# An adaLN transformer block on one core: key-tile sums wholly on GpSimd, earlier loads, and a new order in the first group and the finish

## What is computed

```python
mod = (silu(c) @ wmod).reshape(4, 6, 1, -1)
sa, ca, ga, sb, cb, gb = (mod[:, i] for i in range(6))
ga = sign(ga) * maximum(abs(ga), 0.25)          # gb likewise
h = layernorm(x) * (1 + ca) + sa
x = x + ga * attention(h)                       # causal, softmax(q k / sqrt(32)) v, then Wo and bo
h = layernorm(x) * (1 + cb) + sb
logits = h @ router_w.T                         # 4 experts, the best 2 kept, softmax
x = x + gb * sum_e gate_e * 4 * (h @ A_e.T) @ B_e.T
```

## Time and profile before

| | us |
|---|---|
| median of 3 runs (2901.94 to 2903.45) | 2902.95 |
| the profiled execution | 2904.26 |
| its span | 2902.5 |
| busy: TensorE, VectorE, GpSimd, ScalarE | 2772.0, 1583.7, 1281.9, 1060.7 |
| first attention group from, second from | 1229.5, 1286.4 |
| finish from | 2380.2 |

### The profile page before, as it was taken

The page is one execution under the profiler, slowest core; times in us unless marked ns, Lnnn a source line. Parts: engine busy times, 40 slices in busy tenths (PEclk is TensorE's granted clock), DMA queues, the critical chain, the costliest instruction groups (busy, mean ns, idle before and its releaser), DMA issues. The chain is left out here.

```text
span 2902.5 us, 41782 instructions
## 1 busy us (share of the span) xinstructions
PE 2772.0 (96%) x16195; PEld 2009.4 (69%) x16195; DVE 1583.7 (55%) x3171; ACT 1060.7 (37%) x1449; POOL 1281.9 (44%) x671
## 2 busy tenths in 40 slices
PE   5999999999999999879999999999999978999997
PEld 3888888888888888745555555555555547888886
DVE  4232233222322122267777787888778746777775
ACT  1322222232213111146555566666655641112121
POOL 3322332233224211157777777777777761112120
PEclk8999999999999999979999999999999989999998
DMA  7544354545334644355555555555555545554541
GB/s 250 183 158 159 139 203 166 177 158 190 128 116 149 214 174 175 112 119 125 126 126 124 127 123 121 118 121 119 121 121 128 136 173 142 144 156 136 162 131 58
DMA packets 171709, 421.58 MB, mean 145 GB/s; under 512 B 22204, under 2 KB 74548, under 8 KB 170232
## 3 DMA queue, kind: packets, MB, share of 16 engines
q1 hardware_dynamic: 139240, 298.03, 30.3%
q10 hardware_dynamic: 32272, 120.88, 18.9%
HBM read 278.77 MB, written 139.56 MB: 144 GB/s over the span
## 5 line engine op out<-in xcount | busy, mean ns | idle before, releaser
L1185 ACT ACTIVATE prob<-ps_s 128x1024 f32<-128x1024 f32 (+3 forms) x768 | 597.6, 810 | 415.5 <-PE ps_s L1361 399.8
L846 PE MATMUL ps_u<-h_hi,w_hi 128*128 128x512 f32 x1536 | 612.3, 399 | 1.8 <-POOL h_lo L586 1.8
L846 PE MATMUL ps_u<-h_lo,w_hi 128*128 128x512 f32 x1536 | 600.8, 391 | 0.0
L846 PE MATMUL ps_u<-h_hi,w_lo 128*128 128x512 f32 x1536 | 599.7, 390 | 0.0
L1139 POOL TENSOR_TENSOR added<-added,prob 128x2048 f32<-128x2048 f32 (+1 forms) x128 | 551.5, 4308 | 4.6
L580 POOL TENSOR_TENSOR w_lo<-w_raw,w_hi 128x1024 fp32r<-128x1024 f32 x93 | 222.6, 2393 | 478.4 <-ACT w_hi L648 478.4
L719 DVE SCALAR_TENSOR_TENSOR qk_lo<-ps_u,bias_col,qk_hi 128x512 fp32r<-128x512 f32 x128 | 96.0, 750 | 578.7 <-ACT qk_hi L624 578.7
L1242 DVE TENSOR_REDUCE part_high<-ps_r 128x1 f32<-128x512 f32 x496 | 330.4, 685 | 91.0 <-PE ps_r L1331 90.6
L1238 DVE CUSTOM_DVE_ANT_0 ps_r<-ps_r,row_mask 128x384 f32<-128x384 f32 (+1 forms) x500 | 312.1, 630 | 105.4 <-PE ps_r L1331 104.7
L1331 PE MATMUL ps_r<-k_st,q_st 96*128 96x512 f32 (+1 forms) x1008 | 331.9, 387 | 23.0 <-DMA v_sb<-v_tok 9.5
L846 PEld LDWEIGHTS ps_u<-h_lo,w_hi 128*128 128x128 f32 x1536 | 288.6, 188 | 61.8
(11 more groups left out here) (192 smaller groups left out, 3437.0 us busy)
## 6 DMA issues: line engine op xcount, KB each, us to landing
w_raw<-w_cols SPq DMA_DIRECT2D x72, 512.0 KB, 6.3
qk_split<-qk_hi SPq DMA_DIRECT2D x64, 512.0 KB, 2.6
qk_split<-qk_lo SPq DMA_DIRECT2D x64, 512.0 KB, 4.0
q_st<-qk_split ACTq DMA_DIRECT2D x60, 512.0 KB, 7.5
k_st<-qk_split ACTq DMA_DIRECT2D x60, 512.0 KB, 13.7
xn<-in_L_attn_x SPq DMA_DIRECT2D x8, 2048.0 KB, 11.2
v_tok<-v_out SPq DMA_DIRECT2D x32, 512.0 KB, 4.4
wm<-in_L_wmod SPq DMA_DIRECT2D x8, 2048.0 KB, 8.9
```

The lines of the kernel that those rows point to most:

```text
L846: last = nc.tensor.matmul(ps_u[u % 2][:], w[:, m, k], h[:, k, tok], start=k == 0 and j == 0, stop=k == KT - 1 and j == 2)
L1185: nc.scalar.activation(prob[:, buffer_of(t, k), 2 * pair:2 * pair + 2, off:], ps_s[pair][:, :, off:], ACT.Exp, scale=SCALE).then_inc(exp_d ...
```

## The change

`ADDS` becomes 7: GpSimd adds all eight upper key tiles, the adds of tiles 6 and 7 strewn between the masks 9, 10 and 11, and `sum_high` has only the matmuls on `added`. In the last group only 4 adds are made (`LAST_ADDS`), and matmuls take tiles 5 to 7. Group 1's queries and keys get a place of their own in the room of the projection weights and are loaded in the last group of `project`, the queries at its start, the keys behind the value store. `attend` then loads only values, and `FIRST_SHARE` spreads the 45 row tasks of the first group as 5, then 8 per pair instead of 5, 0, then 10. The gate bounding stands ahead of row task 14 instead of 22. The first four shift DMAs are issued by ScalarE. In the finish VectorE's first chunk has another order, `up_head(0)` on ScalarE follows `split_hi(1)` and the wait for the modulation columns, and TensorE does `project(1, 1)` ahead of `turn(0)`. Other buffers of `finish` (`res`, `at_raw`) move to another address. Left out below: name lists, semaphore and buffer declarations.

```diff
@@ -153,2 +154,4 @@
                 w_hi, w_lo = (weights.enter_context(nc.sbuf_tensor(n, [P, 3, KT, P], F32R)) for n in ("w_hi2", "w_lo2"))
+                slot_1_q = nc.alloc_sbuf_tensor_at("slot_1_q", [QK_ROWS + 1, HG, L], F32R, offset=natural_at)
+                slot_1_k = nc.alloc_sbuf_tensor_at("slot_1_k", [QK_ROWS + 1, HG, L], F32R, offset=natural_at + 4 * HG * L)
                 wo_hi_tile = nc.alloc_sbuf_tensor_at("wo_hi_tile", [P, KT, P], F32R, offset=natural_at + 4 * D)
@@ -158,3 +161,4 @@
             wo_lo = nc.alloc_sbuf_tensor_at("wo_lo", [P, KT, D], F32R, offset=shared)
-            second = -(-nc.sbuf_base // 32) * 32
+            second = natural_at + 8 * HG * L
+            assert -(-nc.sbuf_base // 32) * 32 == natural_at
             wo_hi = nc.alloc_sbuf_tensor_at("wo_hi", [P, KT, D], F32R, offset=second)
@@ -510,2 +515,6 @@
 
+            def load_slot_1(slot, parts):
+                for at, part in parts:
+                    sp.dma_start(slot[at * HD:(at + 1) * HD].bitcast(F32), qk_split[1, part].rearrange("(h d) n -> d h n", d=HD)).then_inc(slot_1_loaded, 16)
+
             for m in range(3):
@@ -523,2 +532,8 @@
                     store_wo(sp, KT - 1)
+                if n == NG - 1:
+                    sp.wait_ge(w_lo_done, 3 * (NG - 1))
+                    sp.wait_ge(wo_stored, 32 * KT)
+                    sp.wait_ge(q_stored, 64)
+                    sp.wait_ge(k_stored, 64)
+                    load_slot_1(slot_1_q, ((0, 0), (1, 1), (2, 0)))
                 if 0 < n < KT:
@@ -551,2 +566,4 @@
                 sp.dma_start(v_tok[n], v_out[:]).then_inc(v_stored, 16)
+                if n == NG - 1:
+                    load_slot_1(slot_1_k, ((0, 2), (1, 2), (2, 3)))
             sp.wait_ge(rows_ready, SEG * KT)
@@ -555,5 +572,2 @@
                 sp.dma_start(dst, rows[32 * j:32 * j + NB]).then_inc(rows_stored, 16)
-            sp.wait_ge(shift_ready, 1)
-            for h in range(HG):
-                sp.dma_start(slot_q[SHIFT_ROW:SHIFT_ROW + 1, h, BANK:2 * BANK].bitcast(F32), shift[1][h * CT:(h + 1) * CT, :].bitcast(F32)).then_inc(shift_loaded, 16)
             store(NG - 1, 2)
@@ -681,2 +695,5 @@
                     split_hi(n, u)
+            act.wait_ge(shift_ready, 1)
+            for h in range(HG):
+                act.dma_start(slot_q[SHIFT_ROW:SHIFT_ROW + 1, h, BANK:2 * BANK].bitcast(F32), shift[1][h * CT:(h + 1) * CT, :].bitcast(F32)).then_inc(shift_loaded, 16)
 
@@ -933,3 +950,4 @@
     RB = 3
-    ADDS = LONG - 3
+    ADDS = LONG - 1
+    LAST_ADDS = FIRST = LONG - CT
     LOW_ADDS = CT - 1
@@ -938,3 +956,2 @@
     MASKS = QC * CT
-    FIRST = LONG - CT
     assert QC == 2 and steps[LONG][1] == 0 and steps[FIRST][1] == CT
@@ -945,3 +962,3 @@
     PLACES = 5
-    FIRST_SHARE = ((1, 1, 1, 1, 1), (0,) * 5) + ((2, 2, 2, 2, 2),) * (PAIRS - 2)
+    FIRST_SHARE = ((1, 1, 1, 1, 1),) + ((2, 2, 2, 1, 1),) * (PAIRS - 1)
 
@@ -989,2 +1006,4 @@
 
+        sb("slot_1_place", [P, 2 * HG * L])
+        assert nc.sbuf_base == second
         slot_2 = [sb(f"{n}_st2", [SHIFT_ROW + 1, HG, L], F32R) for n in "qk"]
@@ -992,4 +1011,3 @@
         v_sb = [sb(f"v_sb{i}", [P, TT, P]) for i in range(SLOTS)]
-        slot_1 = [sb(f"{n}_st1", [SHIFT_ROW + 1, HG, L], F32R) for n in "qk"]
-        q_st, k_st = [slot_q, slot_1[0], slot_2[0]], [slot_k, slot_1[1], slot_2[1]]
+        q_st, k_st = [slot_q, slot_1_q, slot_2[0]], [slot_k, slot_1_k, slot_2[1]]
         inverse = sb("inverse", [P, P])
@@ -1039,3 +1057,3 @@
 
-            return 16 * 7 * (t // SLOTS) + (16 if t % SLOTS == 0 else 16 * 7)
+            return 16 * 7 * (t // SLOTS) + (16 if t % SLOTS < 2 else 16 * 7)
 
@@ -1071,4 +1089,4 @@
 
-            load(sp, 1)
             load_v(sp, 0)
+            load_v(sp, 1)
             for b in range(NB):
@@ -1150,8 +1168,6 @@
                 mask(t, 8)
-                if t < NG - 1:
-                    add(t, 5)
-                mask(t, 9)
-                mask(t, 10)
-                mask(t, 11)
-            add(NG - 1, 5)
+                for k in range(LAST_ADDS + 1, LONG):
+                    if t < NG - 1:
+                        add(t, k)
+                    mask(t, k + CT)
 
@@ -1290,3 +1306,3 @@
                 for n, use in enumerate(strewn(t)):
-                    if t == 0 and n == len(strewn(0)) // 2:
+                    if t == 0 and n == 14:
                         gate_bounds()
@@ -1327,2 +1343,4 @@
                 if use[2:] == high[0]:
+                    if t == 1:
+                        pe.wait_ge(slot_1_loaded, 16 * 6)
                     pe.wait_ge(qkv_loaded[t % SLOTS], loads_upto(t))
@@ -1401,6 +1419,9 @@
                 bank_free(use)
-                pe.wait_ge(added_up, ADDS * (t + 1))
+                adds = ADDS if t < NG - 1 else LAST_ADDS
+                pe.wait_ge(added_up, ADDS * t + adds)
+                if adds < LONG - 1:
+                    pe.wait_ge(masked, masked_upto(t, LONG - 1))
                 for h in range(HG):
-                    nc.tensor.matmul(bank_of(use)[h * HD:(h + 1) * HD, :], ones[:], added[:, h], start=True, stop=False)
-                for k in range(ADDS + 1, LONG):
+                    last = nc.tensor.matmul(bank_of(use)[h * HD:(h + 1) * HD, :], ones[:], added[:, h], start=True, stop=adds == LONG - 1)
+                for k in range(adds + 1, LONG):
                     off = offset(k)
@@ -1676,5 +1697,5 @@
 
-            up_head(0)
             split_hi(1)
             act.wait_ge(mod_ready, 2)
+            up_head(0)
             for n in range(NC):
@@ -1779,2 +1800,8 @@
             nc.vector.tensor_tensor(at_lo[0][:, REST], at_raw[:, REST], at_hi[0][:, REST].bitcast(F32), ALU.subtract).then_inc(first_lo, 1)
+            chain = Chain(dve, dve_chain, tally)
+            dve.wait_ge(bc_loaded, 16)
+            dve.wait_ge(const_ready, 3)
+            residual(0, 0)
+            residual(0, 1)
+            divide(1)
             dve.wait_ge(mod_turned, 1)
@@ -1784,15 +1811,10 @@
             nc.vector.tensor_scalar_add(col[:, :, 1], src[:, :, 1], 1.0).then_inc(mod_ready, 1)
-            dve.wait_ge(bc_loaded, 16)
-            dve.wait_ge(const_ready, 3)
+            layernorm(0, 0)
             scale_up(0)
+            residual(0, 2)
+            residual(0, 3)
+            layernorm(0, 1)
             dve.wait_ge(sums_loaded, 16)
             nc.vector.reciprocal(inv[:], inv[:]).then_inc(inv_ready, 1)
-            chain = Chain(dve, dve_chain, tally)
-            residual(0, 0)
-            divide(1)
-            for u in range(1, UN):
-                residual(0, u)
             up_rest(0)
-            for a in range(T):
-                layernorm(0, a)
             for n in range(NC):
@@ -1892,2 +1914,4 @@
                     go_up(n - 1, range(HV))
+                else:
+                    project(n + 1, 1)
                 turn(n)
@@ -1895,3 +1919,3 @@
                     go_up(n - 1, range(HV, UN))
-                if ahead:
+                if ahead and n > 0:
                     project(n + 1, 1)
```

More of the change, by code:

```diff
@@ L357, in project @@
         s[n] for n in "w_nat w_raw w_hi w_lo row_mask mask_b ident_b max_low part_high max_high shift Wo wo_hi_tile wo_lo_tile wo_split".split())
+    slot_1_q, slot_1_k, slot_1_loaded = (s[n] for n in "slot_1_q slot_1_k slot_1_loaded".split())
     NH = KT * QC
@@ L922, in attend @@
         s[n] for n in "slot_q slot_k row_mask mask_b ident_b max_low part_high max_high shift NB D mod_rows gate_rows att_inv wo_split wo_hi wo_lo wo_ready att_stored sums_stored".split())
-    (at_hi_0, at_lo_0, first_loaded, first_divided, first_hi, first_lo, CW, third) = (
-        s[n] for n in "at_hi_0 at_lo_0 first_loaded first_divided first_hi first_lo CW third".split())
+    (at_hi_0, at_lo_0, first_loaded, first_divided, first_hi, first_lo, CW, second, third, slot_1_q, slot_1_k, slot_1_loaded) = (
+        s[n] for n in "at_hi_0 at_lo_0 first_loaded first_divided first_hi first_lo CW second third slot_1_q slot_1_k slot_1_loaded".split())
     SLOTS = 3
@@ L1479, in finish @@
         inv = sb("inv", [P, HEADS * L // P])
+        res = [sb(f"res{i}", [P, T, D]) for i in range(RES)]
+        at_raw = sb("at_raw", [P, KT, CW])
         up_room = second - nc.sbuf_base
```

3 lines of the change are left out of this document (1 added, 2 removed).

## The result

The changed kernel took **2927.81 us** (median of 4 runs, 2926.6 to 2930.7), the kernel before 2902.62 beside it: a ratio of 1.0086, interval 1.0074 to 1.0098, slower by 25 us. The forecast was 2915, slower by 12, range up to 2925: the direction was right and the meeting that it foretold took place, but its price was too low, and the time lies 3 us outside the range. The profiled execution's span is 2929.0 us against 2902.5. One of all the executions timed, the fourth of the last experiment, was slow (5095 us at a granted clock of 0.544) and is left out of that experiment's figures.

What follows compares the result with a forecast made beforehand. At the attention period's seam VectorE sets TensorE's pace, otherwise TensorE sets everybody's. Terms 21.6 - 10 + 0.5 - 2.5 + 3 = +12.6, rounded to 12, gave 2915 us; likeliest range 2906 to 2925, over all cases 2878 to 2925.

Steps and rivals of the forecast that it cites:

- the meeting: Attention stage, each period: VectorE's first low_total add starts 0.26 us into GpSimd's add 7 and waits 1.00 us.
- The adds: Attention stage: GpSimd's two new adds a group delay TensorE's row 0.72 us a period, +21.6 us in 30 periods.
- The walk: Following one 34.73 us attention period through the engines' timelines; its value of +21.6 us was taken.
- The hold: First low_total add in attention: VectorE waits 1.00 us, until GpSimd's add 7 ends.
- No meeting: Rival for the attention stage: add 7 starts 0.26 us later, VectorE goes first; stage -8.4, total 2885; chance 0.22.
- The exclusive port: Attention adds: VectorE and GpSimd's shared port pair is held whole, not split; by that rule the adds lose.
- busy shares: Attention adds: a reading by engines' busy time alone has moving work from TensorE to GpSimd win 23.9 us.
- Start of attention: First group: waits of 9.46 and 5.15 us go, a gate-bounding stall comes; second group starts at 1276, -10 us.
- the projections' end: End of the projections: the last key stores, on which the barrier waits, queue behind 1.5 MB of loads, +0.5 us.
- End of attention: Last group: without the 1536 add the low_total adds end earlier and TensorE's 4.57 us wait shrinks, -2.5 us.
- Finish: Finish stage: the 5.33 us residual wait goes, but chunk 1 and project(1,2) start later, +3 us.
- The forecast chain: Finish: layernorm(0,0) waits for rsqrt behind at_lo, then residual(0,2), project(1,0); divide(2) moves some 10 us later.

Runs made afterwards that it cites:

- the last experiment: The changed kernel with ADDS 6, the old finish order, slot_1_k loaded behind the last key stores and the gates in the second group: 2874.50 us.
- Experiment 3: The changed kernel with the mask of key tile 11 ahead of add 7 on GpSimd instead of behind it: 2926.28 us.
- Experiments 4 to 6: Changed kernel with ADDS 6, 2889.92 us; that with masks 4 and 5 made twice, 2923.04 us; kernel before with those masks made twice, 2904.63 us.
- the adds alone: The kernel before with only the GpSimd adds moved (ADDS 7, 4 in the last group): 2928.64 us.
- ADDS 6: The changed kernel with ADDS 6 instead of 7, key tile 7 going back to TensorE's sum: 2889.92 us.
- experiment 11: ADDS 6 with the five gate operations on VectorE moved from the first group to the second, behind the first low_total add: 2881.44 us.
- the rest alone: The changed kernel with ADDS back at 5, keeping the early loads, gates' place, shift loads on ScalarE and finish order: 2898.65 us.
- The run with the late load: ADDS 6 with the three loads of slot_1_k issued behind the last store of keys instead of ahead of it: 2887.56 us.
- Experiment 9: ADDS 6 with the finish stage in its old order, the new places of its tiles kept: 2884.99 us.
- the doubled masks: GpSimd's masks of key tiles 4 and 5 made twice: on ADDS 6 2923.04 us, on the kernel before 2904.63 us.

## Why the prediction was right in direction and wrong in size

**The adds, forecast +21.6, measured +26.6 alone and +32.9 in the change's profile.** This is the term that failed: the price of the meeting, "1.00 - 0.28 = 0.72 us" a period. The walk met the right instruction: add 7 in progress under VectorE's first `low_total` add, nothing else in the whole change costing as much. Two things in the price were wrong.
- *The hold.* The forecast had it end with add 7: 1.00 us, the add at 2.7. It ended with the mask behind add 7, and the add took 3.15, a hold of 1.40. The forecast called mask 11 "blocked in turn"; it went first. The upper bound, a hold of all of add 7 (1.26), left the mask out too. Experiment 3 shows that this isn't the mask's doing: an add behind the masks goes ahead of VectorE as well, in 28 of 30 periods.
- *What it means for the period.* The forecast priced the hold against VectorE's path to TensorE, with GpSimd's time fixed by TensorE. Experiments 4 to 6 show the change's bound to be the loop through GpSimd: 30.24 us of work and 5.45 of wait make 35.69, and the size of the hold follows from that. The forecast wrote that GpSimd's wait would be 3 to 4 us, 6.72 less the new work, and so read a wait that ends with VectorE as room. Only 1.27 of the 6.72 was room, with 0.89 and 0.27 more ahead of the masks:

```profile
1723.42 0.64 POOL L1121 TENSOR_SCALAR_AFFINE_SELECT prob<-prob 128x512 f32<-128x512 f32 x1 [0.27 <-ACT prob L1185]
```

That is 2.43 us in all, and the new adds are 3.6. Had I written the loop down, the rows of before would have given GpSimd's work of 26.85 us and the stretch from VectorE's first `low_total` add to GpSimd's next add, 5.71 (1742.87 to 1748.58): with 3.63 of new adds 36.2 us, and 35.9 with the 5.45 that the later runs show.

That +21.6 lies as near as it does is partly luck. The forecast took the base from one period, 34.73, where the mean of the 30 is 34.95, and the period at 35.45, where the floor is 35.69; the two errors cancel, and from the mean to the floor is +22.2. The other 10.7 of the +32.9 are what the periods lie over the floor: 4.3 in the one at the lower clock, the rest in periods where GpSimd waits for an exponent besides. With the adds alone that part is 4.4 in all. The forecast had no term for it.

**No meeting**, the rival at 2885 with chance 0.22, did not come: the first `low_total` add was held in each of the 30 periods. Its deciding point, 0.26 us in the phase of add 7, was not what decides, since GpSimd's own lateness sets the phase. In the two periods of experiment 3 in which VectorE did go first, the period was 35.33 and 34.73, not under 34.6. That ADDS 6 takes 2889.92, near the rival's 2885, is no hit for it: there the work is less.

**The exclusive port.** The rule that I weighed from the Trainium skill (SBUF — State Buffer, section "SBUF: two separate sides") agrees with the traces: 1.40 us of hold in the change, and 4.50 and 4.29 us for gate operations that take 0.22 where GpSimd waits (experiment 11). That busy shares mislead here was right too: from the rest alone (2898.65) to the change (2927.81) is +29 us, for 3.7 us more of GpSimd's work a period, on an engine that was busy 44%.

**Start of attention, forecast -10 and +0.5, measured -8.5 together.** Both waits went, the stall behind the gates was 9.5 us. The second group's start came 9.0 us earlier (1277.38 against 1286.39) although the stage itself began 3.8 later, SP's first transfer at 1233.20 instead of 1229.4. So the stage's own part is -12.8, better than -10, and the projections' end +3.8, above its bound of +2. The step that was mis-sized is "queue behind 1.5 MB: +0.5". The run with the late load puts its size at 5.5 us on the barrier; from the kernel before it is +3.8 only, since the last stores are issued 1.5 us earlier than there (1223.49, they were at 1224.99).

**End of attention, forecast -2.5, measured -2.9.** TensorE's last wait for `low_total` is 1.47 us instead of 4.57.

**Finish, forecast +3, measured +5.0.** The forecast chain is in the timeline: `rstd` behind GpSimd's `at_lo`, VectorE's `xn` at 2437.48 after 4.86 us of waiting, the residual behind it, `project(1,0)` at 2441.75, and `divide(2)` at 2460.54 after 10.32 us for its transfer. Experiment 9 gives the 5 us back.

## What to carry to other kernels

When work is moved to an engine that waits in each period, ask what ends that wait. If the wait ends with a chain that itself begins when this engine lets go, write the loop down (its own work plus the chain) and compare it with the period: only the difference is room, and past it each microsecond of work in the loop costs a microsecond a period, as add 7 did and as the doubled masks did 15 us away from it. Then move in small steps: of the two adds moved here, the first alone gained 9 us, and both together cost 29.

Small operations that share a port with long ones belong where the long ones wait anyway (11.0 us became 1.8 here); and loads put ahead of the stores that a barrier waits for make the barrier later (5.5 us for 1.5 MB here).

## What the runs showed of the hardware that I had not expected

- VectorE's waiting `low_total` add seldom gets in between two back-to-back GpSimd instructions, whether a mask follows an add (began at 1745.95, GpSimd's last end 1746.09; so in all 30 periods of the change) or an add follows masks (1745.56 and 1745.69; so in 28 of 30, and in two it got in). It begins 0.13 to 0.14 us before the recorded end of the one that held it.
- The small gate operations did get in: L1293 between an add and a mask, L1294, with two inputs in SBUF, between that mask and the next add. So it is not a rule that GpSimd's ready instruction goes first; what decides is open.
- Gate operations with a single SBUF input (L1293, L1295) were held as well, 4.50 and 4.29 us for 0.22 us of work.
- With the loads of 1.5 MB ahead of them the last stores held the barrier 5.5 us longer, although they were issued within 0.6 us of the same time.
- With the `low_total` adds behind rows 1, 2 and 3 in the changed kernel TensorE's granted clock fell in 23 of 30 periods (0.97 over the stage); with the same places and ADDS 6 it fell in none.
